# A transformer stack in one kernel: a fourth set of score stacks, V copied by ScalarE, and the max row sent by ScalarE

## The reference

```python
x = x + _L0_xattn_ref(_layernorm(x), ctx_1024, mask, ...)   # cross attention, self attention, dense FFN, each with its output layer norm
x = x + _L0_ffn_ref(_layernorm(x), ...)                     # top-2 routing over 8 experts, one of them a no-op
x = x + _L1_xattn_ref(_layernorm(x), ctx_1024, ctx_1024, ...)
x = x + _L1_ffn_ref(_layernorm(x), ...)                     # half of the tokens through an FFN
...
q = _split_heads(x @ qw + qb)
k = _split_heads(ctx @ kw + kb)
v = _split_heads(ctx @ vw + vb)
scores = jnp.einsum('bqhd,bkhd->bhqk', q, k) / np.sqrt(D // H)
if mask is not None:
    scores = scores + mask
probs = jax.nn.softmax(scores, axis=-1)
out = jnp.einsum('bhqk,bkhd->bqhd', probs, v)
...
h = h @ w + b          # the output projection
```

## Time and profile before

| what | us |
|---|---|
| median of 3 runs | 943.43 |
| lowest, highest | 942.08, 1312.43 |
| the profiled execution | 937.4 |
| its span, first to last instruction | 935.7 |
| TensorE busy | 775.4 (83%) |
| VectorE busy | 556.4 (59%) |
| ScalarE busy | 424.9 (45%) |
| GpSimd busy | 410.9 (44%) |

### The profile page before, as it was taken

One profiled execution on the slowest core, in us unless ns is written; L12 is line 12 of the kernel. 1 busy time (PEld: TensorE's weight loads), 2 busy tenths in 40 slices (PEclk: granted clock), 3 DMA queues, 4 the chain that ended last, 5 costly groups with the idle time before them and its releaser, 6 DMA issues.

```text
span 935.7 us, 16978 instructions
## 1 busy us (share of the span) xinstructions
PE 775.4 (83%) x6612; PEld 632.8 (68%) x6612; DVE 556.4 (59%) x1164; ACT 424.9 (45%) x708; POOL 410.9 (44%) x421
## 2 busy tenths in 40 slices
PE   4578999999999879999762699992467999779897
PEld 4456767777777548999762588881355767548896
DVE  5557988887888744556746011202577998755432
ACT  3145666666676666556420111220124667564232
POOL 8634574542365345544686311005865356124200
PEclk9779999999999999999965799996559999999999
DMA  8985798857885502300250462361577985500011
GB/s 191 167 126 84 120 125 117 124 85 110 106 122 77 75 1 91 113 2 1 70 177 12 148 206 87 57 146 57 109 111 96 126 103 72 70 2 2 23 34 34
DMA packets 77115, 83.72 MB, mean 89 GB/s; under 512 B 8910, under 2 KB 72397, under 8 KB 76992
## 3 DMA queue, kind: packets, MB, share of 16 engines
q1 hardware_dynamic: 73786, 76.44, 45.7%
q0 software_dynamic: 3072, 6.04, 2.6%
q10 hardware_dynamic: 178, 0.16, 0.0%
HBM read 36.70 MB, written 10.11 MB: 50 GB/s over the span
## 4 chain that ended last, share of the span: by engine, by line
PE 54%; DVE 12%; DMA 11%; SPq 8%; POOL 6%; issue 5%; ACT 3%; POOLq 0%; DVEq 0%; ACTq 0%
SPq L395 7%; PE ps L186 7%; PE ps L187 6%; PE ps L188 6%; DVE nmax L1256 6%; PE ps L714 6%; PE ps L551 5%; PE ps L728 5%; DMA kst<-mask_dram 4%; DMA kst<-k_parts 4%; PE ps L767 3%; PE ps L613 3%; PE ps L573 3%; PE ps L777 3%; PE ps L210 2%
## 5 line engine op out<-in xcount | busy, mean ns | idle before, releaser
L1256 DVE TENSOR_REDUCE nmax<-ps 128x4 f32<-128x1024 f32 x192 | 234.7, 1224 | 86.6 <-PE ps L551 84.6
L850 ACT ACTIVATE prob<-ps 128x1024 f32<-128x1024 f32 x192 | 196.2, 1022 | 78.2 <-PE ps L573 75.6
L1023 POOL TENSOR_TENSOR rstd<-var,half 128x2 f32<-128x2 f32 x56 | 41.2, 735 | 276.7 <-DVE var L1196 217.9
L551 PE MATMUL ps<-kst,qst 50*128 50x256 f32 (+1 forms) x768 | 99.5, 340 | 44.9 <-DVE nmax L1256 29.9
L551 PEld LDWEIGHTS ps<-kst,qst 50*128 50x128 f32 (+1 forms) x768 | 60.4, 195 | 90.1 <-DVE nmax L1256 58.8
L613 PE MATMUL ps<-prob,vext 128*32 128x256 f32 x1536 | 104.6, 390 | 0.6 <-ACT oext L863 0.6
L573 PE MATMUL ps<-qst,kst 51*128 51x256 f32 (+1 forms) x768 | 82.3, 293 | 16.0 <-ACT prob L850 9.7
L573 PEld LDWEIGHTS ps<-qst,kst 51*128 51x128 f32 (+1 forms) x768 | 61.3, 192 | 22.7 <-ACT prob L850 13.6
L1116 POOL DMA_INDIRECT gat<-moe_out,slu x32 | 35.5, 1109 | 72.6 <-DMA moe_out<-vext 63.9
L613 PEld LDWEIGHTS ps<-prob,vext 128*32 128x32 f32 x1536 | 40.7, 110 | 31.4 <-issue 3.5
L1027 POOL TENSOR_SCALAR hres<-xres,mv,rstd 128x256 f32<-128x256 f32 x48 | 59.0, 1234 | 2.6
(11 more groups left out here) (218 smaller groups left out, 2075.7 us busy)
## 6 DMA issues: line engine op xcount, KB each, us to landing
kst<-k_parts SPq DMA_DIRECT2D x144, 128.0 KB, 6.3
qst<-q_parts SPq DMA_DIRECT2D x144, 128.0 KB, 4.6
e_in<-in_ein SPq DMA_DIRECT2D x5, 1024.0 KB, 5.3
e_out<-in_eout SPq DMA_DIRECT2D x5, 1024.0 KB, 8.9
ctx_raw<-in_ctxT SPq DMA_DIRECT2D x16, 256.0 KB, 7.3
ew_in<-in_ein SPq DMA_DIRECT2D x2, 1024.0 KB, 5.9
ew_out<-in_eout SPq DMA_DIRECT2D x2, 1024.0 KB, 8.5
out<-xres SPq DMA_DIRECT2D x8, 256.0 KB, 2.1
```

The lines of the kernel that those rows point to most:

```text
L551: last = pe.matmul(score_pair(n, p)[:, 512 * s + S * t:512 * s + S * (t + 1)], qst[j][a:b, p, t * P:(t + 1) * P], kst[j][a:b, p, :], start ...
L850: act.activation(probs[p % 4][:].rearrange("p i t s -> p (i t s)"), T_PS, ACT.Exp).then_inc(sm["exp_done"], 1)
L1256: dve.tensor_reduce(nmax[n % 2][:, :, :, p].rearrange("p t s -> p s t"), score_pair(n, p).rearrange("p (s t k) -> p s t k", s=2, t=TB), AX ...
```

## The change

There are six edits.

1. A fourth set of stacks for items 0 to 15. It lies where `fi_hi` and `fi_lo` are loaded later, so items 12 to 15 use sets 0, 1, 2, 0 again and the chunks of the second FFN matrix are now loaded ahead of those of the first. Items 16 to 23 keep three sets. V keeps three buffers.
2. ScalarE sends the max row, one DMA with 16 source partitions and two destination rows, right behind its own copy into `m_hi`. SyncE no longer waits for it.
3. The mask rows are a program of their own on SyncE, ahead of the keys and queries, and the queries' stack has two halves, the first due 1.5 steps earlier for items with a fourth set free.
4. V is copied by ScalarE in one instruction, without its bias. For each layer TensorE multiplies the V bias with the output weights in four matmuls and VectorE adds this to the bias row of the projection (`out_bias`).
5. The columns of query and key weights are ordered so that a stack's block of 16 rows comes from 64 partitions with two slots of 256 each, where it came from 128 partitions with one slot. A stack is still six DMAs of 128 KB.
6. Due times of some programs move: the transposes of the queries 1.2 steps earlier, some layer-norm steps by 1 to 2 steps.

```diff
+        _, kst3, qst3 = overlay([("fill_s", [P, 18432]), ("kst3", KS, F32R), ("qst3", KS, F32R)])
+        kst, qst = stacks[0::2] + [kst3], stacks[1::2] + [qst3]
...
+        SET = [n % 4 for n in range(12)] + [0, 1, 2, 0] + [n % 3 for n in range(NA, 3 * B)]
+        BIAS_AT = (3.1, STEP * 5 + 2.9, T_C0 - 9.3)
...
-        T_CHUNK = [6 + 9 * i for i in range(8)] + [STEP * B + 30 + 9 * i for i in range(4)] + [T_E0 + 5 + 3 * i for i in range(4)]
+        T_CHUNK = [6 + 9 * i for i in range(4)] + [STEP * B + 18.5 + 5 * i for i in range(4)] + [STEP * B + 43 + 6 * i for i in range(4)] + [T_E0 + 5 + 3 * i for i in range(4)]
...
-                def stack(n, which):
-                    j = n % NSET
+                def stack(n, which, halves=(0, 1)):
+                    j = SET[n]
                     dst = qst[j] if which == "q" else kst[j]
-                    for s in range(2):
+                    for s in halves:
                         for c in range(3):
-                            sp.dma_start(dst[64 * s + DH * c:64 * s + DH * (c + 1), :, :].bitcast(F32), PARTS[which][c][:, s, :].bitcast(F32)).then_inc(sm[f"stk_{which}{j}"], 16)
+                            sp.dma_start(dst[64 * s + DH * c:64 * s + DH * (c + 1), :, :].bitcast(F32), PARTS[which][c][64 * s:64 * s + 64, :, :].bitcast(F32)).then_inc(sm[f"stk_{which}{j}"], 16)
...
+                def stack_mask(n):
+                    j = SET[n]
+                    yield start_of(n) - 8.5 if n > 1 else -5 - n
+                    if n >= 4:
+                        sp.wait_ge(sm["st_ps"], HG * (last_user(n) + 1))
...
                 def stack_q(n):
-                    j, t0 = n % NSET, start_of(n)
-                    yield t0 - 6.8
+                    j, t0 = SET[n], start_of(n)
+                    yield t0 - (8.3 if n and n - (last_user(n) or -9) > 3 else 6.8)
...
-                    stack(n, "q")
-                    yield t0 + (8.1 if lead(n) else 8.9)
-                    sp.wait_ge(sm["m_row"], n + 1)
-                    for s in range(2):
-                        r = 64 * s + max_row(n)
-                        sp.dma_start(qst[j][r:r + 1, :, :].bitcast(F32), m_hi[HG * s:HG * (s + 1), :].bitcast(F32)).then_inc(sm[f"stk_m{j}"], 16)
+                    stack(n, "q", (0,))
+                    yield t0 - 6.8
+                    stack(n, "q", (1,))
...
@@ TensorE
-                    yield t0 - 13.4
+                    yield t0 - (14.6 if n not in (0, NA) else 13.4)
...
+                def out_bias(a):
+                    yield BIAS_AT[a]
...
+                    for i in range(2 * KD):
+                        k, half_w = i // 2, W[a][3][i % 2]
+                        last = pe.matmul(bias_bank(a), cols[:, 6 + a, k:k + 1].to_broadcast([P, P]), half_w[:, k, :].bitcast(F32),
+                                         start=(i == 0), stop=(i == 2 * KD - 1))
+                    last.then_inc(sm["bo_ps"], 1)
...
@@ ScalarE
+                def values(n):
+                    yield kv_start(n) - (4.15 if n not in (NA, NA + 1) else 4.35)
+                    j = n % VSET
+                    act.wait_ge(sm["v_ps"], n + 1)
...
+                    act.activation(vext[j][:, :, :, 0:DH], G[1].rearrange("p (t h d) -> p t h d", t=TB, d=DH), ACT.Copy).then_inc(sm["v_ready"], 1)
+
                 def attention(n):
...
                     act.activation(m_hi[:], PV_PS[0:H, 0:S], ACT.Copy).then_inc(sm["m_row"], 1)
+                    r = max_row(n)
+                    act.wait_ge(sm["m_row"], n + 1)
+                    act.dma_start(qst[SET[n]][r:r + 65:64, :, :].bitcast(F32), m_hi[:].bitcast(F32)).then_inc(sm[f"stk_m{SET[n]}"], 16)
...
@@ GpSimd
-                    for j in range(NSET):
+                    for j in range(4):
                         yield -14 + 8 * j
...
@@ VectorE
+                def out_bias(a):
+
+                    yield BIAS_AT[a] + 1.2
...
+                    row = rows[:, R_OUT[a], :]
+                    dve.tensor_tensor(row, bias_bank(a), row, ALU.add).then_inc(sm["bo_s"], 1)
...
@@ host
-        return w.reshape(-1, 2, HG, DH).transpose(0, 1, 3, 2).reshape(w.shape)
+        return w.reshape(-1, 2, HG // 2, 2, DH).transpose(0, 3, 1, 4, 2).reshape(w.shape)
```

More of the change, by code:

```diff
@@ L106, in build @@
         half = sb("half", [P, 2])
-        vext = [sb(f"vext{j}", [P, TB, H, 2 * DH]) for j in range(NSET)]
+        vext = [sb(f"vext{j}", [P, TB, H, 2 * DH]) for j in range(VSET)]
         probs = [sb(f"prob{r}", [P, 2, TB, S]) for r in range(4)]
@@ L220, in xb, with users, last_user @@
             return xres[:, TB * (n % B):TB * (n % B) + TB, :]
+        SET = [n % 4 for n in range(12)] + [0, 1, 2, 0] + [n % 3 for n in range(NA, 3 * B)]
+        def users(n):
+            return [i for i in range(n + 1) if SET[i] == SET[n]]
         def used(n):
-            return n // NSET + 1
+            return len(users(n))
+        def last_user(n):
+            return users(n)[-2] if used(n) > 1 else None
         ITEMS = range(3 * B)
@@ L612, in pv @@
                             p, s = 2 * u + i // 2, i % 2
-                            last = pe.matmul(half_bank[32 * i:32 * i + 32, :], vext[n % NSET][:, t, s * HG + p, :],
+                            last = pe.matmul(half_bank[32 * i:32 * i + 32, :], vext[n % VSET][:, t, s * HG + p, :],
                                              probs[p % 4][:, s, t, :], start=(t == 0), stop=(t == TB - 1),
@@ L784, in mod @@
                     last.then_inc(sm["upd_ps"], 1)
-                side_by_side(*(queries(n) for n in ITEMS), *(keys_values(n) for n in ITEMS), *(attention(n) for n in ITEMS),
+                side_by_side(*(queries(n) for n in ITEMS), *(keys_values(n) for n in ITEMS), *(out_bias(a) for a in range(3)), *(attention(n) for n in ITEMS),
                              *(ffn(f) for f in range(B)), *(route(g) for g in range(len(GROUPS))), *(expert(e) for e in range(NE)),
@@ L1289, in attention @@
                         dve.tensor_tensor(flat(res[:]), G[2], flat(hb(n)), ALU.add).then_inc(sm["res_s"], 1)
[L1290 removed]
+                        yield t0 + later(n, 26.6)
                         dve.wait_ge(sm["res_s"], n + 1)
[L1292 removed]
+                        yield from slow_stats(res, 1, t0 + later(n, 28.6), sm["ln_var"])
                 def ffn(f):
@@ L1445, in _ @@
                 side_by_side(setup(), mask_rows(), first_weights(), second_stacks(), *(queries(n) for n in ITEMS),
-                             *(split(n, "k", kv_start(n) - 7.4 if n else -14.3) for n in ITEMS), *(values(n) for n in ITEMS),
+                             *(split(n, "k", kv_start(n) - 7.4 if n else -14.3) for n in ITEMS), *(out_bias(a) for a in range(3)),
                              *(attention(n) for n in ITEMS), *(ffn(f) for f in range(B)), *(route(g) for g in range(len(GROUPS))),
@@ L1483 @@
         "rowC": _np.stack([g[c + "b_v"], g[c + "b_o"], g["L1_ffn_b2"], g["L1_ffn_w_router"]]),
+        "colV": _np.stack([col(g[n]) for n in (a + "cv_b", a + "sv_b", c + "b_v")], axis=1),
         "w1": g["L1_ffn_W1"], "w2": g["L1_ffn_W2"], "b1": col(g["L1_ffn_b1"]),
```

149 lines of the change are left out of this document (77 added, 72 removed).

## The result

The changed kernel took 965.19 us in the median of five runs (963.54 to 972.42, the highest being the profiled one), the kernel before 946.56 beside it. The ratio of the fast runs (which leave out the one of 1312.43 us) is 1.0236, with an interval of 1.0197 to 1.0275; the two medians alone give 1.020. So the change is slower, by some 2.4%. The forecast was 935 and its range ended at 953. The span of the profiled execution is 970.7.

What follows compares the result with a forecast made beforehand. TensorE was taken as the bound in steady items, VectorE pacing some periods. Terms -8.9 - 3.9 + 1.0 - 2.0 + 5.3 = -8.5 took the profiled 937.4 to 928.9, plus 6.0 to the median: 935; range 918 to 953.

Steps and rivals of the forecast that it cites:

- The landing of the max row: Max row's arrival in the query stack: one DMA saves an issue but has two destination rows; set at nothing.
- C: Rival: max row lands late behind stack packets in flight, 2.1 us more per item, 44 in all, 979; chance 0.08.
- ScalarE's issue: Max-row DMA issue on ScalarE, 0.61 us, delays the next exponential; TensorE stalls 0.35 in 15 items, +5.3, bounds 0.6 and 11.
- rival A: Rival: ScalarE's issue costs nothing, 929.6; with a compact start too, 923; chance 0.23.
- Stack waits: TensorE's waits for stacks: 5.5 us of the eleven periods and more at the blocks' last items gone, together -8.9.
- and the 2.0: TensorE's wait at the first scores of the first block's last item: all 2.0 us taken as gone.
- the 1.4 for SyncE's two issues: Second cross layer, still three sets: SyncE saves two max-row issues, winning 1.4 of a 2.3 us wait.
- D: Rival: the keys' split still releases the last six copies, so 8.9 shrinks to some 3, 941; chance with B 0.19.
- V off VectorE: V copied by ScalarE without bias: VectorE saves 0.77 us in each of five periods it paces, -3.9; ScalarE's copy hidden.
- The bias: V bias moved into the output row: four matmuls per layer, counting in the middle layer's full period, +1.0, at worst +3.
- Packets of 2 KB: Stack copies with 64 packets in place of 128 speed the opening, where DMA is full: -2.0, bounds 0 and -2.6.
- B: Rival: the halves cancel, ScalarE's issue costing 11 and V's copy not fully hidden, 943; chance with D 0.19.

Runs made afterwards that it cites:

- e8_hold: The changed kernel with SyncE holding its later stack copies until the max row, still sent by ScalarE, has landed; 947.29 us, ratio 1.0008.
- e2_sync: The changed kernel with the max row back on SyncE, at its old place and in two DMAs, all other edits kept; 937.20 us, ratio 0.9900.
- e11_hold_swap: The changed kernel with SyncE's later copies held until the row has landed and ScalarE issuing the row behind the exponential; 934.02 us, ratio 0.9885.
- e9_sync_vdve: e2_sync with the V copy back on VectorE in two instructions, still without bias; 942.20 us, ratio 0.9960.
- e13_holdrow: The changed kernel with SyncE's later copies waiting only for ScalarE's copy of the max row, not its landing; 946.54 us, ratio 1.0007.
- e5_1kb: The changed kernel with the old column order, so stack copies have 1 KB packets, ScalarE still sending the row; 980.19 us, ratio 1.0364.

## Why the prediction was wrong

The lengths below are differences of the starts of the max-row copies in the profiled executions, one of each kernel. The one of the kernel before (937.4) lies 6 us under the median of its first three runs, the one of the changed kernel (972.42) is the highest of five, so they are 35 us apart where the medians are 18.6. The 1st to the 3rd copy is the first block's edge, the 3rd to the 14th the eleven periods of the prediction, the 17th to the 19th the second block's edge.

| kernel | 1st to 3rd | 3rd to 14th | 17th to 19th |
|---|---|---|---|
| before | 44.0 | 207.1 | 43.4 |
| after | 50.9 | 219.4 | 53.4 |
| e8_hold | 43.9 | 208.8 | 47.7 |
| e2_sync | 42.6 | 202.8 | 46.0 |

**The landing of the max row failed: "I set it at nothing, with the rival below".** That step was mis-sized by 18 us (medians of after and e8_hold) to 22 (their ratios), most of the miss. The rival below, C, had the mechanism right. It put the limit at 3.4 us from issue to need, ScalarE's stall included. In e8_hold the score that needs the row starts 4.06 us after the issue (215.68 against 211.62), since the stall is longer and moved transposes stand ahead of it (without the stall it starts 3.92 after the copy in e2_sync, where it was 3.48). A steady landing takes 4.39, so 0.33 too long. With the score itself at 0.51 in place of 0.40 that is most of the 0.5 by which the period is longer than e8_hold's (19.29 against 18.78). At the edges, where little covers the row, 1.95 became 4.9 to 6.4, and the table has 7.1 and 5.6 us there against e8_hold. Part of that is the clock: the second period's 164 matmul instructions kept TensorE busy for 19.98 us at a granted clock of 0.79, and for 17.28 at 0.91 in e8_hold. C took a landing of 5.5 us for every item and so came to 44 where 18 to 22 was measured: in the middle of a block slack takes most of it. What went wrong is C's chance. The reason against it was that the row "is small and on a queue of its own". Its own queue did not protect it here: 16 KB on ScalarE's queue landed late behind the 128 KB copies of SyncE's. What had protected the row was SyncE's order, in which bulk came after it, and the change took that away along with the stall that it meant to remove. The text had seen this ("Today SyncE's queue is empty when it is issued. After the change the stack's packets are in flight") and still let the size decide.

The Trainium skill says as much (DMA: Bandwidth & Descriptors, "Issuing engines are not separate DMA queues"): DMAs from different issuing engines run on the same 16 DMA engines and interleave. The traces agree: 1.94 us with SyncE held, 4.4 to 6.4 without. The rule that the prediction did draw on, how many engines a DMA gets, was the wrong one for this: with the same two destination rows the landing with SyncE held is 1.94, against 1.95 for SyncE's form.

**ScalarE's issue: right in mechanism, short in size.** Predicted: 0.61 of issue, the exponential starting 1.00 after the copy's start and 0.35 of stall in 15 items, +5.3. Measured: issue 0.51, the exponential after 1.02. The stall is 0.5 per steady item (18.78 against 18.27), 6.0 us in the eleven full periods (208.8 against 202.8). The whole costs more: e8_hold is 10.1 above e2_sync, and e11_hold_swap, which differs from e8_hold in the order alone, is below it by 1.2% of the time. So the term is 10 to 12 and near the bound of 11; where the 4 to 6 us outside the full periods lie, single profiles don't show. The slack of 0.37 would leave 0.35 or so of it; the first transposed score behind it also took 0.50 where it took 0.40 before, and that may be the rest. The Trainium skill's figure of some 50 ns for the dispatch stands in an account of DMAs issued by GpSimd (DMA: Bandwidth & Descriptors, "Anatomy of one DMA — SWDGE (gpsimd) path"), so it could not carry rival A. ScalarE here is held for 0.51 us, unless an activation already runs.

**Stack waits: 5.5 came, 3.4 didn't.** In e2_sync the eleven periods take 202.8, of which 1.8 are bias matmuls: 201.0, where 201.6 was the floor I had set. The waits of 2.0 and 2.3 at the blocks' last items are 2.4 and 2.0 in e2_sync, 2.6 and 1.7 in the changed kernel. The step "and the 2.0" failed: items 12 to 15 have sets 0, 1, 2, 0, so item 15 takes the set of item 12, three back, as before. In the changed kernel SyncE waits 19.0 us for those scores ahead of the queries' stack of item 15, and the keys, split at 324.75, go out behind it:

```profile
325.95 3.76 SPq L415 DMA_DIRECT2D qst<-q_parts  x6
329.81 3.76 SPq L415 DMA_DIRECT2D kst<-k_parts  x6
```

In the second cross layer it is the same (keys split at 828.41, issued at 833.76), so of the 1.4 for SyncE's two issues 0.6 came. D named the keys' split as the last release; at both places it is these scores and the six copies of the queries. In the steady periods D fell.

**V off VectorE** was -3.9, measured -5.0 (e9_sync_vdve), with intervals that overlap. That it was gained where VectorE paces is not shown: the waits for maxima fell from 29.9 in the kernel before to 19.4 in the changed one, but with V back on VectorE they stay at 22.5, against 22.7. So the size agrees and the place is open. ScalarE's copy was indeed hidden: 0.59 us each, and no engine waited for it.

**The bias** was +1.0 and is +1.8 in the full period. Four matmuls per layer were counted, by the code; the trace shows 24 instructions at line 546, eight per layer, and eight by the 0.24 of a like one is 1.9. **Packets of 2 KB** were -2.0 and are nothing that can be measured (0.9900 against 0.9890).

**The sum.** The forecast stood 8.5 below the profiled execution, the measured medians are 18.6 apart the other way: 27 to explain. The landing gives 18, the exponential 5 to 7, the block ends 3.4, the packets 2.0, the bias 0.8, and V takes 1.1 back: 28 to 30. The terms are medians of different chips and single profiles. By the ratios to the kernel before on the same chip, in us of some 944, the change is at +22, e8_hold at +1, e2_sync at -9. So the landing cost 22 (forecast 0), ScalarE's issue 10 (forecast 5.3), and all other edits gave -9 (forecast -13.8), which makes a miss of 31.

Rival A (the issue is free) fell with e8_hold. B (the halves cancel) gives e8_hold's number, 1.0008, but in part by luck, for V's copy, which B had exposed, was hidden; it does not describe the change. The prediction's own sign for C, "TensorE waiting on qst from m_hi by over 1 us", is what the profile showed.

Two losses had no term. The second block's edge takes 2.6 more in e2_sync than before; the row lands in 3.2 us there by its chain (at 687.23), and in 4.3 just behind it (733.21), though SyncE sends it. And the opening up to the first max-row copy, which the table leaves out, took 49.23 us before and 53.00 in the changed kernel, 52.23 in e2_sync, 50.59 in e13_holdrow. The prediction had it 2.0 shorter; single executions don't say why it isn't.

Left open: what 1 KB packets add when ScalarE sends the row (e5_1kb); how the row's delay divides between copies ahead of it and beside it at the edges; and what the fourth set and the moved due times (edit 6) are worth by themselves.

## What to carry to other kernels

A small DMA that is awaited can be held up by a bulk stream on another engine's queue (1.94 us became 4.4 to 6.4 here). Before moving the small one to a "free" queue, ask what the old place in the order kept away from it, and if it must move, let the bulk wait for its landing: one wait was worth some 20 us here. And a DMA issue on ScalarE held up its next instruction but ran beside one already started, so put it behind a long one. The two together made the best version (0.9885), where each of them by itself (1.0008 and 1.0198) looked like a dead end.

## What the runs showed that I had not expected

- A 16 KB row between partitions lands in 1.94 us with SyncE's copies held back and in 4.4 to 6.4 behind them; at a steady item one DMA of two rows took 4.39 and the second of two DMAs of one row 4.87.
- ScalarE's sequencer issues a DMA in 0.51 us. The next activation started 0.74 us later than without it (1.02 against 0.28 after the copy's start), while one started 0.12 us before the issue runs on untouched, at its 1.00 us.
- Twice as many bytes per packet in the stack copies left the kernel's time as it was (0.9900 against 0.9890), in a kernel whose DMA share is 0.6 to 0.7 in the full periods.
- A later landing at an edge came with a lower clock. In the second period the granted clock was 0.79 with the row landing in 6.17 us, and the period took 24.89, TensorE being busy for 19.98 of it. In e2_sync it was 1.00, as before, and the period took 17.81 (a stretch of e2_sync, columns as above):

```profile
76.98:94.79 17.81, 15.76 (x164) 11.87 (x165) 14.46 (x24) 10.87 (x19) 8.17 (x9) 1.00 0.75 119
```
